# A graph layer kernel in ten blocks: how the engines meet at the end of each block

## What is computed

```
edge_index = jnp.stack([src, dst])
xn = _layernorm(x, axis=-1)
x = x + _L0_gnn_ref(xn, ...) + _L0_mix_ref(xn[None], ...)[0]      # relational graph attention, linear attention
x = x + _L0_ffn_ref(_layernorm(x)[None], ...)[0]                  # shared expert + 2 of 8 routed experts
xn = _layernorm(x, axis=-1)
x = x + _L1_gnn_ref(xn, ...) + _L1_mix_ref(xn[None], ...)[0]      # two graph convolutions, linear attention and MLP
x = x + _L1_ffn_ref(_layernorm(x)[None], ...)[0]                  # top-k routed FFN (gelu), the rest passes through
```

## Time and profile before

| | us |
|---|---|
| median of 3 runs | 2839.17 |
| lowest, highest | 2838.43, 2846.54 |
| the profiled execution | 2842.59 |
| its span, first to last instruction | 2840.8 |
| its mean granted TensorE clock | 0.891 |

### The profile page before, as it was taken

One profiled execution on the slowest core, in us unless ns is written; L12 is line 12 of the kernel. 1 busy time (PEld: TensorE's weight loads), 2 busy tenths in 40 slices (PEclk: granted clock), 3 DMA queues, 4 the chain that ended last, 5 costly groups with the idle time before them and its releaser, 6 DMA issues. The chain is left out here.

```text
span 2840.8 us, 42657 instructions
## 1 busy us (share of the span) xinstructions
PE 2288.4 (81%) x11329; PEld 1709.0 (60%) x11329; DVE 1314.0 (46%) x3509; ACT 1076.3 (38%) x2885; POOL 1376.8 (48%) x1407
## 2 busy tenths in 40 slices
PE   6899847767777988999997797777754798886898
PEld 5454534445455876888886465455544676764577
DVE  6553456766676130111113332343239666666851
ACT  3333544544441212233333443255420655553211
POOL 0221477777730051122221577777767777776300
PEclk9999867888788899999998898988775899999899
DMA  3476644444411024777774433344547444443300
GB/s 98 157 217 221 182 110 122 119 120 119 120 53 36 16 90 145 204 223 195 210 216 138 139 106 106 105 128 124 158 111 254 137 132 150 132 130 97 108 14 32
DMA packets 249527, 374.45 MB, mean 132 GB/s; under 512 B 66472, under 2 KB 186740, under 8 KB 249322
## 3 DMA queue, kind: packets, MB, share of 16 engines
q0 software_dynamic: 70000, 179.80, 22.9%
q1 hardware_dynamic: 132740, 140.88, 16.3%
q10 hardware_dynamic: 46582, 51.38, 5.4%
HBM read 298.68 MB, written 73.27 MB: 131 GB/s over the span
## 5 line engine op out<-in xcount | busy, mean ns | idle before, releaser
L2794 POOL DMA_INDIRECT cm_rows<-rows,e_bsrc x392 | 373.0, 952 | 175.5 <-issue 96.9
L1182 POOL DMA_INDIRECT store<-rows,e_bsrc x392 | 378.6, 966 | 119.4 <-issue 109.0
L1529 POOL DMA_INDIRECT at_rows<-values,e_brow x362 | 344.3, 951 | 115.1 <-issue 89.3
L1609 PE MATMUL at_part<-at_msg,store 128*128 128x265 f32 x880 | 269.7, 449 | 86.1 <-DVE at_msg L1765 42.2
L2931 PE MATMUL cm_part<-cm_rows,cm_one 128*128 x880 | 264.7, 443 | 88.9 <-SPq L2807 58.9
L1209 PE MATMUL banks<-ag_msg,ag_one 128*128 128x258 f32 x880 | 227.3, 396 | 67.8 <-issue 44.7
L2931 PEld LDWEIGHTS cm_part<-cm_rows,cm_one 128*128 128x128 f32 x880 | 179.8, 218 | 157.5 <-issue 134.2
L1609 PEld LDWEIGHTS at_part<-at_msg,store 128*128 128x128 f32 x880 | 175.8, 218 | 156.6 <-DVE at_msg L1765 65.5
L2231 POOL DMA_INDIRECT x_sum<-x_y,x_target x56 | 87.1, 1555 | 340.7 <-DVE x_y L2344 333.4
L3147 DVE TENSOR_TENSOR store<-store,cm_part 128x256 f32 x220 | 92.2, 419 | 339.7 <-PE cm_part L2931 311.7
L1209 PEld LDWEIGHTS banks<-ag_msg,ag_one 128*128 128x128 f32 x880 | 164.5, 194 | 114.9 <-issue 56.3
(11 more groups left out here) (700 smaller groups left out, 3923.7 us busy)
## 6 DMA issues: line engine op xcount, KB each, us to landing
x_w<-in_L_ffn_W1p SPq DMA_DIRECT2D x32, 1024.0 KB, 5.2
x_w<-in_L_ffn_W2p SPq DMA_DIRECT2D x32, 1024.0 KB, 5.5
values<-at_rows ACTq DMA_DIRECT2D x25, 1088.0 KB, 5.9
p_brow<-local_row SPq DMA_DIRECT2D x44, 320.0 KB, 4.1
xn_acc<-low_row SPq DMA_DIRECT2D x28, 448.0 KB
expert_in<-store POOLq DMA_DIRECT2D x7, 1040.0 KB, 8.3
at_rows<-values,e_brow POOLq DMA_INDIRECT x392, 2.8
cm_rows<-rows,e_bsrc POOLq DMA_INDIRECT x392, 2.7
```

The lines of the kernel that those rows point to most:

```text
L1182: pool.indirect_dma_start(rows[:, b % slots, k, :], None, table, bass.IndirectOffsetOnAxis(index[:, k, b:b + 1], 0)).then_inc(gathered[b % ...
L1529: pool.indirect_dma_start(rows[:, b % RING, k, :], None, table, bass.IndirectOffsetOnAxis(e.block_row[:, k, b:b + 1], 0)).then_inc(gathere ...
L1609: last = pe.matmul(part[:, bank["pair", n], 0:wide], one[:, n // U % 2, k, n % U, :], msg[:, n % 4, k, :], start=(k == 0), stop=(k == K2 - 1))
L2794: pool.indirect_dma_start(rows[:, b % SLOTS, k, :], None, table, bass.IndirectOffsetOnAxis(e.block_src[:, k, b:b + 1], 0)).then_inc(gather ...
```

## The change

```diff
@@ together
-        with nc.Block() as block:
+        with nc.Block(no_gpsimd_drain=True) as block:
             TOGETHER.append((block, sems, memories))
             yield
             TOGETHER.pop()
         nc.clear_and_free_semaphores(sems)
-        nc.all_engine_barrier()
+        nc.all_engine_barrier(sem_only=True)
```

## The result

The changed kernel takes 2824.78 us, the median of six runs, against 2842.35 us for the kernel before in the same comparison: a ratio of 0.9935, with a 95% interval from 0.9919 to 0.9951. That is 0.65% faster, or 18.5 us by the ratio (the two medians lie 17.6 us apart). It is rival A of the prediction, the reset DRAIN that doesn't wait for DMAs, and its price of 18.5 us agrees with the measured ratio.

What follows compares the result with a forecast made beforehand. Only the ten block ends matter, with POOL's emptying last at four; the reset DRAIN takes over its wait. -1.2 - 0.6 + 0.5 = -1.3 us brings the median from 2839.2 to 2837.9, range 2833 to 2851.

Steps and rivals of the forecast that it cites:

- rival A: At the block ends, the reset DRAIN doesn't wait for DMAs: 18.5 us gained, 2820.7 us; chance 0.12.
- What bounds: Only the ten block ends matter; at ends 3, 6, 8 and 9 POOL's DRAIN comes last to the first meeting.
- the prize: At ends 3, 6, 8 and 9, 18.8 us of the span are POOL's DRAIN and nothing else.
- what the reset DRAIN takes: Between the two meetings, it takes over the whole wait of POOL's removed block-end DRAIN, leaving a gain of 1.2 us.
- rival B: At the ends, a DRAIN starts a job, which the reset DRAIN now does exposed: +10.4 us, 2849.6 us; chance 0.22.
- The DRAIN of the second meeting: POOL's DRAIN there goes, on the path at all ten ends: gain 0.4 to 0.7, taken 0.6 us.
- the separate arrivals: At the first meeting, arrivals become instructions, on the path at six ends: loss 0.3 to 0.7, taken 0.5 us.
- Rival C: Behind the ends, shifted phases and code addresses move the time up to 8 us either way; chance beyond some microseconds 0.10.
- The sign of the forecast: Over the whole kernel, slightly faster: -1.3 us, with -2.1 to -0.4 at the ends.

Runs made afterwards that it cites:

- the probe: A program of its own: POOL issues gathers, then a plain or reset DRAIN in several settings; behind 32 landed gathers 2651 ns plain, 73 ns reset.
- the DRAIN in the open: The changed kernel with a plain POOL DRAIN put back behind the first meeting at all ends: 2854.69 us, ratio 1.0043 to the kernel before.
- the second half alone: Kernel before with only the second meeting changed to semaphores alone, POOL's DRAIN at the block's end kept: 2841.23 us, ratio 0.9995.
- the first half alone: Kernel before with only POOL's DRAIN at the block's end removed, the second meeting keeping its DRAINs: 2821.87 us, ratio 0.9942.
- the four ends: Kernel before with the whole change at ends 3, 6, 8 and 9 alone, the other six as before: 2820.03 us, ratio 0.9918.
- the probes: Two programs of POOL gathers followed by DRAINs, the second with more counts: plain DRAIN 126 ns behind one gather, 9.18 us behind 112.

## Why the prediction was wrong

**What bounds, and the prize: right in the main.** The four ends and the engine that came last at each were read correctly. The saving at the ends is 17.1 us. It is less than the prize of 18.8 since at end 3 POOL still issues gathers until 352.4 while DVE is done at 350.0; the prediction counted the whole 5.6 us of that end as the DRAIN's, and 3.5 were to be had. That slip belongs to rival A's sum too: it gave 18.5 for the mechanism, where its own row of POOL's last gather would have given some 16.5. That the ratio comes to 18.5 as well is thus partly luck; its interval, 0.9919 to 0.9951, is 14 to 23 us and holds both.

**The step that failed: what the reset DRAIN takes.** The prediction bounded it by 0.1 us and by the whole wait and took the second, so that only 1.2 us were left to gain there. The runs showed the first: nine of the ten took 0.08 to 0.20 us, and the one at end 3 took 2.19 us for POOL's own instructions. The prediction had two grounds: the short times in the earlier trace rows all lie behind an emptied POOL, and the Trainium skill's rule ("PSUM — Partial Sum Buffer", "Engine vs sequencer instructions") that a drain waits for the engine to go fully idle. The first ground only said that the rows were silent; it didn't favour either end. Beside them stood a reading, that the reset DRAIN is the same instruction with a range of semaphores added, which took for granted what was to be settled. As for the rule: the reset DRAIN did wait for POOL's instructions (2.19 us at end 3, and 15.0 us in the probe), so the rule holds as far as the instructions go. Of DMAs under way it says nothing by name: the reset DRAIN didn't wait for them and the plain one did (L97 and L78 of the probe), and the plain one does a job besides. The one number that spoke for a second mechanism, the 6.5 to 9.2 us between the last DMA instruction and the DRAIN's end, at ends 8 and 9 with a DMA share of 0.00, stood in the prediction, under rival B. A wait for idleness shouldn't last while nothing is seen under way; a job was the likelier reading, and a job can belong to one kind of instruction and not to another. That should have lifted rival A well above 0.12.

**The smaller terms.** The DRAIN of the second meeting, taken at 0.6 us for ten ends, and the separate arrivals, taken at 0.5 us against it: the second half alone saves 0.5 us at the ends. The six other ends cost the same to 0.03 us before and after, so the two terms cancel there, as the sum had it.

**Rival B: right in its mechanism, wrong in the instruction.** Most of a long plain DRAIN's time is a job that it starts. Its argument against itself (at ends 2 and 3 the DRAIN ended 2.1 and 3.6 us behind the last gather, too short for a fixed job) falls with the size: the job isn't fixed, it goes by the number of DMAs. The 2.1 us at end 2 fit a wait for the landing of its two gathers; with the DRAIN in the open, long behind the landing, it took 0.22 us. The kernel with the plain DRAIN in the open measured 0.43% slower where rival B had 0.37%. That these are so near is partly luck: rival B had 2.1 us at end 2 and nothing at end 9, where the DRAIN in the open cost 5.9 us more than before.

**Rival C** got 0.10 and neither shows in the medians nor is ruled out below some 4 us: the whole change twice gave 0.9935 and 0.9934, the first half alone 0.9942, the four ends 0.9918. All four times lie below what the end costs explain, by 1 to 7 us; for three of them this is within the interval, for the four ends it is just outside. Whether the blocks gain a microsecond or two, for instance from the shorter idling ahead of them, stays open.

**The chances.** The sign of the forecast was right. Its size was off by a factor of fourteen, and the range left out rival A with the whole of its 0.12, though it had a worked-out time and nothing but an unsettled reading against it.

## What to carry to other kernels

Where a program is cut into blocks that end in a meeting of all engines, look at the DRAIN rows of each end one by one and ask who comes last; on POOL, a plain DRAIN behind n of its own DMAs costs about 0.05 + 0.08 n us up to 112 DMAs, even when all have landed long ago, so either leave it out where the data are waited for by semaphores (the reset DRAIN that stays doesn't wait for them) and the semaphores' clearing has its own reset DRAIN, or put it where POOL has time. When an instruction's time isn't explained by what it waits for, take that as a sign of work of its own, and give the case that this work goes with the instruction a chance of its own size.

## What the runs showed of the hardware that I had not expected

- The two kinds of DRAIN on POOL differ by up to 9 us. Behind 32 landed DMAs they take 2651 and 73 ns, and after the reset kind the plain one takes 46. With data under way, the plain kind waits for the landing and the reset kind doesn't.
- The plain kind's price is linear in the number of POOL's DMAs, 126 ns at 1 and 9184 ns at 112, whatever their kind, and falls back between 112 and 120: in the probes POOL pauses for 3.8 us before the 114th gather since the last DRAIN, and then before every 128th.
- A program's executions can differ by 16 us in span with the same code (2810.7 and 2826.7), nearly all of it inside the blocks and 10.8 us of it in two long ones.
